# First block of a four-layer kernel: the context's load is issued ahead of the positions', and the rotation table's store is no longer awaited by the block that issues it

## The reference

```python
x = x + _L0_xattn_ref(ctx_1024, _layernorm(x, axis=-1), ...)   # state-space scan over ctx, gated by x
x = x + _L0_ffn_ref(_layernorm(x, axis=-1), ...)               # 4-bit weights
x = x + _L1_xattn_ref(_layernorm(x, axis=-1), ctx_1024, fside_BxSx2_0, fside_BxSx2_0, ...)  # attention, rotated by position
x = x + _L1_ffn_ref(...)
x = x + _L2_xattn_ref(_layernorm(x, axis=-1), ctx_1024, ...)
x = x + _L2_ffn_ref(...)
x = x + _L3_xattn_ref(ctx_1024, _layernorm(x, axis=-1), ...)   # scan again
x = x + _L3_ffn_ref(...)
```

```python
x = jnp.einsum('ed,bld->bel', in_proj_w, hidden_states)      # hidden_states is ctx_1024
xc = jax.lax.conv_general_dilated(xp, conv_w[:, None, :], ...)
u = jax.nn.silu(xc + conv_b[None, :, None])
x_dbl = jnp.einsum('ke,bel->bkl', x_proj_w, u)
```

```python
ang = pos[..., :, None] * freqs
cos = jnp.cos(ang)[:, :, None, :, :]
sin = jnp.sin(ang)[:, :, None, :, :]
```

## Time and profile before

| | |
|---|---|
| median of 3 runs | 4228.2 us (4226.68 to 4228.35) |
| the profiled execution, its own time | 4224.04 us |
| its span | 4222.2 us |
| mean granted TensorE clock | 0.923 of full speed |
| busy share of the span: PE, DVE, ACT, POOL | 85%, 70%, 42%, 36% |
| first stage | 0 to about 29.4 us of the span |

### The profile page before, as it was taken

One profiled execution on the slowest core, in us unless ns is written; L12 is line 12 of the kernel. 1 busy time (PEld: TensorE's weight loads), 2 busy tenths in 40 slices (PEclk: granted clock), 3 DMA queues, 4 the chain that ended last, 5 costly groups with the idle time before them and its releaser, 6 DMA issues. The chain is left out here.

```text
span 4222.2 us, 46653 instructions
## 1 busy us (share of the span) xinstructions
PE 3601.3 (85%) x15115; PEld 1721.6 (41%) x15163; DVE 2957.5 (70%) x4169; ACT 1763.2 (42%) x2945; POOL 1503.5 (36%) x1038
## 2 busy tenths in 40 slices
PE   5788764999999999898999879785877887689898
PEld 2233322555555555442333344333333332244454
DVE  4889988588777884457888266527667899844663
ACT  3555541222222221243777453327664555421254
POOL 2999863122211220054000100004436999800122
PEclk7899887999999999997999989896998888889999
DMA  3455441121333212366774110001005455412420
GB/s 106 131 144 140 122 139 54 49 80 59 94 101 99 73 34 76 116 144 99 80 79 49 53 60 0 3 8 65 0 0 143 135 138 133 127 47 69 79 54 22
DMA packets 249831, 338.33 MB, mean 80 GB/s; under 512 B 45603, under 2 KB 147523, under 8 KB 248037
## 3 DMA queue, kind: packets, MB, share of 16 engines
q1 hardware_dynamic: 249620, 335.70, 32.0%
HBM read 284.38 MB, written 53.35 MB: 80 GB/s over the span
## 5 line engine op out<-in xcount | busy, mean ns | idle before, releaser
L701 ACT ACTIVATE m_dA<-m_delta,m_a_neg 128x512 f32<-128x512 f32 x512 | 349.9, 689 | 473.3 <-DVE m_H_bank L794 386.5
L553 PE MATMUL m_y<-m_H,ident 128*128 128x512 f32 x512 | 307.3, 689 | 180.0 <-DVE m_H L811 179.9
L1899 DVE TENSOR_REDUCE a_core_minus_max<-a_core_a 128x1 f32<-128x512 f32 x512 | 317.1, 683 | 57.6 <-PE a_core_a L1725 57.6
L733 POOL TENSOR_TENSOR m_dB<-m_du,m_BC 128x1024 f32<-128x1024 f32 x128 | 315.6, 2466 | 44.5 <-DMA m_BC<-bc_ready 33.3
L561 PE MATMUL m_y<-m_H,ident 128*128 128x512 f32 x512 | 298.3, 674 | 34.7 <-POOL m_H L715 34.7
L715 POOL TENSOR_TENSOR m_H<-m_H,m_BC 128x512 f32<-128x512 f32 x224 | 300.1, 1340 | 45.3 <-DVE m_H L803 45.2
L1851 ACT ACTIVATE X<-a_core_s 128x512 f32<-128x512 f32 x512 | 264.6, 603 | 93.1 <-PE a_core_s L1725 93.0
L733 POOL TENSOR_TENSOR XN<-m_du,m_BC 128x1024 f32<-128x1024 f32 x128 | 300.9, 2356 | 2.7 <-DMA m_BC<-bc_ready 2.7
L1291 POOL TENSOR_TENSOR ctxT<-ctxT,f_scales 128x1024 f32<-128x1024 f32 x48 | 105.9, 2206 | 532.8 <-DVE ctxT L1116 532.8
L1357 DVE SCALAR_TENSOR_TENSOR XN<-f_u,f_power_back,XN 128x512 f32<-128x512 f32 x128 | 95.8, 748 | 232.2 <-PE f_u L1188 232.2
L1251 ACT ACTIVATE XN<-f_g,f_power_back 128x512 f32<-128x512 f32 x128 | 88.0, 687 | 404.2 <-PE f_g L1188 404.2
(11 more groups left out here) (411 smaller groups left out, 8352.7 us busy)
## 6 DMA issues: line engine op xcount, KB each, us to landing
m_BC<-bc_rows SPq DMA_DIRECT2D x224, 512.0 KB, 4.8
XN<-in_L_ffn_w_dram SPq DMA_DIRECT2D x72, 256.0 KB, 2.7
m_BC<-bc_ready SPq DMA_DIRECT2D x32, 512.0 KB, 5.0
ternary<-ctxT SPq DMA_DIRECT2D x96, 128.0 KB, 1.7
a_core_q<-a_q_parts SPq DMA_DIRECT2D x48, 256.0 KB, 12.8
a_core_k<-a_k_parts SPq DMA_DIRECT2D x48, 256.0 KB, 14.6
f_w_tern<-ternary SPq DMA_DIRECT2D x24, 512.0 KB, 5.9
f_core_q<-f_q_parts SPq DMA_DIRECT2D x24, 512.0 KB, 8.2
```

What stands on the lines that cost most here:

```text
L553: pe.matmul(ps_y[:, 0, :], ident[:], HD[n % NH], start=False, stop=True, skip_group_check=True).then_inc(s_ad, 1)
L701: act.activation(dA[:, i % NA, :], delta[b % 2][:, e, :], ACT.Exp, scale=a_neg[:, e, k % N:k % N + 1]).then_inc(s_dA, 1)
L733: pool.tensor_tensor(dB[n % ND][:], du[b % 2][:, h * EH:(h + 1) * EH, :], BC[n % NS][:, 0:1, :].broadcast_to([P, EH, L]), ALU.mult).then_i ...
L1899: dve.tensor_reduce(mx[u % 2][:, qt, h:h + 1], ps_a[:, at % NR, 0:n], AX.X, ALU.max, negate=True).then_inc(s_red, 1)
```

## The change

The change touches the first stage and two waits of later ones:

- The load of the context is SP's first instruction of the stage, ahead of the wait for the zeroed tiles and of the four loads of positions and frequencies.
- The tile `rope_table` of the first stage is gone; the sine is written to the first 256 columns of tile 4 of `XN`, and stored from there.
- The store counts on a semaphore that belongs to the chip object and not to the stage, so it lives on. SP doesn't wait for it in the first stage.
- Two later places wait for it: ACT before the gates of batch 1 in the first scan (the first writer of tile 4), and SP in `stage_ffn4` ahead of reading the table.

```diff
@@ Chip.__init__
+        self.rope_stored = nc.alloc_semaphore("rope_stored")
@@ stage_start
-        ang, turns, tab = (chip.sb("rope_" + n, [P, 2, P], F32, st) for n in ("angle", "turns", "table"))
+        ang, turns = (chip.sb("rope_" + n, [P, 2, P], F32, st) for n in ("angle", "turns"))
+        tab = chip.XN[:, TB, 0:2 * P].rearrange("p (s t) -> p s t", s=2)
@@ block.sync of stage_start
+            sp.dma_start(cn[:], ctx_dram.rearrange("b (t p) c -> p (b t) c", p=P)).then_inc(s_c, 16)
             sp.wait_ge(s_zero, 2)
             for a in range(A):
...
-            sp.dma_start(cn[:], ctx_dram.rearrange("b (t p) c -> p (b t) c", p=P)).then_inc(s_c, 16)
             weights.load_rows(sp)
             weights.load_small(sp)
             sp.dma_start(X[:], x.rearrange("b (t p) c -> p (b t) c", p=P)).then_inc(chip.loaded, 16)
             sp.wait_ge(s_sin, 1)
-            sp.dma_start(table.rearrange("s q t -> q s t"), tab[:]).then_inc(s_tab, 16)
-            sp.wait_ge(s_tab, 16)
+            sp.dma_start(table.rearrange("s q t -> q s t"), tab).then_inc(chip.rope_stored, 16)
@@ block.scalar of stage_start
-            act.activation(tab[:], ang[:], ACT.Sin).then_inc(s_sin, 1)
+            act.activation(tab, ang[:], ACT.Sin).then_inc(s_sin, 1)
@@ gates(b) in stage_mamba
                 act.wait_ge(norm.s_sh, 1)
+                if then and b == 1:
+                    act.wait_ge(chip.rope_stored, 16)
@@ block.sync of stage_ffn4
             load(sp, 1)
+            sp.wait_ge(chip.rope_stored, 16)
```

More of the change, by code:

```diff
@@ L135, in stage_start @@
         s_rt, s_rc, s_rate, s_zero = (chip.sem("rope_" + n) for n in ("turned", "posT", "rates", "zeroed"))
-        s_ang, s_ch, s_red, s_sin, s_tab = (chip.sem("rope_" + n) for n in ("angle", "chain", "reduced", "sin", "stored"))
+        s_ang, s_ch, s_red, s_sin = (chip.sem("rope_" + n) for n in ("angle", "chain", "reduced", "sin"))
         s_c = chip.sem("start_ctx")
```

## The result

| | before | after |
|---|---|---|
| median of 12 runs each | 4222.9 us (4217.43 to 4228.35) | 4214.57 us (4208.55 to 4222.77) |
| ratio of the runs | | 0.9984, 95% interval 0.9976 to 0.9992 |
| the profiled execution, its span | 4224.04, 4222.2 us | 4213.80, 4212.0 us |

The change gains 0.16%, 6.8 us by the ratio (3.4 to 10.1 by its interval); the plain difference of the two medians is 8.3 us. That is clear of zero and still under the 0.2% set at the start. The forecast was a gain of 6.7 us, and a time of 4221.5 us in a range of 4216.5 to 4226.5. The median of before that the forecast stood on, 4228.2 of 3 runs, is 4222.9 over 12.

What follows compares the result with a forecast made beforehand. The first block's end was taken as set by the table's store landing behind `X`, 9.1 us after everything else. With ACT ending later, at 22.6, the gain was 6.7 us: 4228.2 - 6.7 = 4221.5 us, range 4216.5 to 4226.5.

Steps and rivals of the forecast that it cites:

- The wait at the block's end: End of first block: SP's 9.2 us wait for the rotation table's store goes; worth 9.1 us if ACT's end stayed.
- The barrier does not wait for transfers in flight: End of first block: the second stage can start while `X`, landing near 29, is still loading.
- rival B: End of first block: the barrier holds while `X` is in flight, gain 0, time 4228; chance 0.06.
- T: First stage: time when positions and frequencies are there, 6.0 before, expected 12.0 behind the held issues.
- Rival A: First stage: positions less late (T 10.7, gain 8.0) or clock stays up (another 2.2); gain 8.5 us or more; chance 0.26.
- Sine at 16.7, last copy 22.6, first matmul 24.0: First stage's end: sine 4.7 us after T, copies 5.9 us, then 1.4 us to PE's first matmul, before at 30.68.
- Rival C: First stage: positions starved, T 15.3, first matmul 27.3, gain 2 to 4 us, time 4224.8; chance 0.08.
- the way out and in: Between first and second stage: leaving and entering the blocks takes 1.4 us, 1.26 before.
- The copies at the lower clock throughout: First stage, by the skill: transposes don't count for the clock gate, ACT ends at 23.6, gain 5.7 us.
- The clock, 0: Second stage's start: PE's clock changes nothing, 0 us; +2.2 if it stays high, -1 if it returns later.
- D: Projections and convolution: clock stays at 0.50, 18.4 us more against 6.7 won, time 4239.9; chance 0.04.
- Sum: 4228.2 - 6.7: Whole kernel: median of the runs before, less the forecast gain, gives 4221.5 us.

Runs made afterwards that it cites:

- e1: Changed kernel with the loads in the old order (positions and frequencies, then context), store still not awaited; ratio 0.9980 to the kernel before, median 4212.45 us.
- e2: Changed kernel with the wait for the table's store put back at the end of the first block; ratio 1.0005 to the kernel before.
- e5: Changed kernel with frequencies first, then both position axes in one load that a DVE copy unpacks; one execution, 4214.93 us.
- e7: Changed kernel with e3 and e5 together, sine table loaded at the start, sine ahead of the last two copies; ratio 0.9971 to before, median 4206.75 us.
- e3: Changed kernel with PE turning context before positions, ACT's sine behind the eight copies, store issued ahead of `X`; ratio 0.9979 to the kernel before.

## Why the prediction was right about the change and wrong about the time

- *The wait at the block's end goes, and nothing else takes its place but ACT*: right. SP's queue is free at 16.92 + 3.51 = 20.43, ACT's last copy ends at 22.77. e1 and e2 show that the wait is the whole gain.
- *The barrier does not wait for transfers in flight*: right, and rival B is out. `X` lands at 29.3, and the second stage starts at 23.9.
- *T, the positions' landing, 12.0*: measured 12.2, with the second positions' issue at 9.15 (expected about 9). The mechanism, an issue queue held behind the context, shows in the queue's rows and again in e5. (Rival A's T of 10.7 is 1.4 us behind the context's 9.3, and not the "about 2" that it is said to be.)
- *Sine at 16.7, last copy 22.6, first matmul 24.0*: measured 16.89, 22.77, 23.90. Rival C would have put the last at 27.3. That the last agrees to 0.1 us is in part luck: the way out and in took 1.13 us and not 1.4, which makes up for copies that ended 0.17 late, and over all profiles of the two kernels the mean head moved by 7.2 us (31.14 to 23.95), not 6.8.
- *The copies at the lower clock throughout, ACT's end at 23.6*: this did not happen. Nothing but transposes ran on PE from 13.94, and eight weight loads took 1.57 us at 17.41 and 0.91 at 21.00, as they had gone from 1.57 to 0.94 before.
- *The clock, 0*: right within what it scatters. It fell between 22 and 24 and was back at about 34, four us after the projections began, as before:

```profile
22.00:24.00 2.00, 0.25 (x3) 0.13 (x2) 0.06 (x1) 0.91 (x3) 0.00 (x0) 0.93 1.04 386
...
32.00:34.00 2.00, 2.00 (x4) 0.83 (x3) 2.00 (x4) 0.17 (x1) 0.00 (x0) 0.51 0.00 0
34.00:36.00 2.00, 2.00 (x6) 0.87 (x5) 2.00 (x4) 0.76 (x2) 0.00 (x0) 1.00 0.00 0
```

These windows are length, busy of PE, PEld, DVE, ACT, POOL, granted clock, DMA share and GB/s, as in the earlier trace rows. The 9.10 us of the projections against 9.11 are luck to that digit: they take 9.11, 10.14 and 9.59 us in the three profiles of before, and 9.10 and 9.43 in the two of the changed kernel. Both parts of rival A failed: the queue was held, and the clock fell though PE stood idle for only 1.75 us before L461. (In e7 it fell between 20 and 22, a granted clock of 0.91 there, with PE busy for all of that stretch and for 0.37 of the 2 us before it.) Of D nothing showed.

- *"Sum: 4228.2 - 6.7"*: this is the step that failed. The 6.7 us were right within what the runs can tell (6.8, interval 3.4 to 10.1), and the number that they were taken from was 5.3 us too high: 4228.2 instead of 4222.9. The three runs shown lay between 4226.68 and 4228.35, and I read their spread of 1.7 us as the kernel's. The nine other runs of that comparison lie between 4217.43 and 4224.41, with a median of 4220.63; over all 56 runs of the kernel before the median is 4221.7, and only five are over 4226, three of them these three. The profiled execution said so already: 4224.04, 4.2 us below the median, in the table of times. I noted the difference and did not ask what it meant for the width of the range. That range, 4216.5 to 4226.5, stands for gains of 1.7 to 11.7 us from 4228.2: it goes only 1.5 us beyond rival A's 10.2, and holds nothing for an error of the base. From 4222.9 the same sum gives 4216.2, which would itself lie 0.3 us below the range and 1.6 above the result; from the profiled execution it gives 4217.3, inside the range and 2.8 above the result. The last 1.6 us are no more than the changed kernel's own scatter: its median was 4214.57 in the first series and 4218.13 in the second.
- Where the scatter sits: for the most part in the stages behind the head. Over the ten profiles the first scan's length goes over 5.7 us (573.5 to 579.2, from the first matmul to the memset of `f_xnT_norm_eps`), the second layer's attention over 4.1, the others over 1 to 3. The two profiles of the changed kernel (578.1 and 579.2) lie at before's upper end (575.5 to 578.3), e1 and e3 (576.5, 575.6) at its lower, so no order goes with the kernels, but for e7, whose 573.5 is the lowest. What makes it is open: no run here separates it, and none was made to. Why the first three runs were all high is open too.

## What to carry to other kernels

In this kernel a wait on a store that was issued behind a large load was a wait on that load; take such a wait to the first reader, and look for what sat just behind it. A large load moved to the head of the queue held back the issues behind it, also those that the next engine asks for first. Where the consumers kept the old order this cost 2.4 us (e1 against the changed kernel). Where they took the new one the cost was taken back (e3), and the move paid only with the other repairs of e7, 1.8 us over e1. And when a change is worth less than the kernel's scatter, forecast the difference, and take the base and its width from every execution that there is, the profiled one among them.

## What was not expected

- The issue of an 8 KB load was held for 5.47 us on SyncE behind a 2 MB load and 2048 single elements, and that of the first weights for 4.80 us (4.44 to 9.24) in e7.
- The block was left with 4 MB in flight to a tile that the next stage reads: the first matmul came 5.4 us ahead of the landing at 29.3, with 1.1 us from the last copy's end to it (22.77 to 23.90; 20.32 to 21.46 in e1).
- A sine placed behind the copies brought a second table load into the stage (1.28 us at 17.69 in e3), where the sine ahead of the copies needed one load for both.
